# Attribute rows of two chunks side by side in a ring of 50 units: a graph network on one core

## The reference, cut to what matters

```python
for i in range(L):                       # L = 3
    q, k, v = x @ Wq[i] + bq[i], x @ Wk[i] + bk[i], x @ Wv[i] + bv[i]
    e = edge_attr_64 @ We[i]
    alpha = sum(q[dst] * (k[src] + e), -1) / sqrt(64)
    w = segment_softmax(alpha, dst)
    x = segment_sum((v[src] + e) * w[:, None], dst) + x @ Ws[i] + bs[i]
    x = relu(x)                          # and layer_norm for i < 2
...
msg = norm[:, None] * (concat([x[row], edge_attr_32], 1) @ weight)   # third layer
```

## Time and profile before

| | |
|---|---|
| median of three runs | 4897.83 us |
| the profiled execution's own time | 4912.25 us |
| its span, first to last instruction | 4910.5 us |
| mean granted TensorE clock | 0.794 |
| first gather of convolutions 0, 1, 2 | 97.8, 1285.8, 2478.2 us |
| last product of convolution 2 | 3592.6 us |

### The profile page before, as it was taken

The page is one execution under the profiler, slowest core; times in us unless marked ns, Lnnn a source line. Parts: engine busy times, 40 slices in busy tenths (PEclk is TensorE's granted clock), DMA queues, the critical chain, the costliest instruction groups (busy, mean ns, idle before and its releaser), DMA issues. The chain is left out here.

```text
span 4910.5 us, 91838 instructions
## 1 busy us (share of the span) xinstructions
PE 3513.1 (72%) x24220; PEld 3047.3 (62%) x24220; DVE 3256.5 (66%) x10240; ACT 2423.5 (49%) x8504; POOL 2498.9 (51%) x2591
## 2 busy tenths in 40 slices
PE   3677766666667666666657778777846999964887
PEld 2555555555555555555546667777746999962787
DVE  7677776777567776777737777777763333324996
ACT  0766666665376666666456666665421000000554
POOL 5777777674477777777267777777511000000000
PEclk9777888998578888988757888888757999975555
DMA  3444444442334444444144444444222000000001
GB/s 78 101 102 105 101 119 117 118 123 72 84 92 101 103 112 116 119 118 121 35 105 98 101 98 104 105 106 101 65 81 104 2 2 2 1 21 7 2 3 23
DMA packets 596225, 389.26 MB, mean 79 GB/s; under 512 B 441290, under 2 KB 518210, under 8 KB 595720
## 3 DMA queue, kind: packets, MB, share of 16 engines
q1 hardware_dynamic: 392839, 156.12, 12.5%
q0 software_dynamic: 81344, 84.68, 9.9%
q10 hardware_dynamic: 121536, 142.57, 9.8%
HBM read 315.36 MB, written 67.70 MB: 78 GB/s over the span
## 5 line engine op out<-in xcount | busy, mean ns | idle before, releaser
L615 POOL DMA_INDIRECT arena<-node_table,arena x1660 | 1603.2, 966 | 612.6 <-issue 467.8
L770 PE MATMUL ps<-arena 128*128 128x129 f32 x4980 | 948.3, 321 | 184.6 <-DVE arena L920 102.0
L679 ACT ACTIVATE arena<-arena 128x129 f32<-128x129 f32 x2490 | 742.8, 301 | 456.9 <-DVE arena L888 452.1
L770 PEld LDWEIGHTS ps<-arena 128*128 128x128 f32 x4980 | 791.0, 226 | 270.9 <-DVE arena L920 137.0
L917 DVE TENSOR_SCALAR arena<-arena 128x128 f32<-128x128 uint16 x2490 | 883.2, 360 | 94.7 <-PE ps L770 41.8
L615 POOL DMA_INDIRECT arena<-last_node_table,arena x830 | 794.1, 957 | 290.0 <-issue 233.5
L888 DVE TENSOR_TENSOR arena<-ps,arena 128x258 f32<-128x258 f32 x1245 | 524.3, 421 | 590.0 <-PE ps L759 247.9
L1165 PE MATMUL ps<-arena 128*128 128x192 bf16 x6875 | 589.6, 247 | 56.0 <-PEq L86 40.3
L1165 PEld LDWEIGHTS ps<-arena 128*128 128x128 bf16 x6875 | 587.4, 98 | 58.1 <-issue 52.3
L759 PE MATMUL ps<-arena,e 128*128 x2484 | 498.4, 332 | 113.4 <-DVE arena L888 56.5
L759 PE MATMUL ps<-arena 128*128 x2496 | 499.4, 333 | 103.6 <-ACT e L669 33.0
(11 more groups left out here) (324 smaller groups left out, 4705.8 us busy)
## 6 DMA issues: line engine op xcount, KB each, us to landing
arena<-in_attr SPq DMA_DIRECT2D x1245, 96.0 KB, 2.3
arena<-slot_rows ACTq DMA_DIRECT2D x249, 320.0 KB
edge_counts<-al ACTq DMA_DIRECT2D x397, 100.0 KB
arena<-node_table,arena POOLq DMA_INDIRECT x1660
edge_counts<-stage ACTq DMA_DIRECT2D x198, 100.0 KB
arena<-last_node_table,arena POOLq DMA_INDIRECT x830
arena<-edge_counts SPq DMA_DIRECT2D x24, 500.0 KB
stage<-edge_counts SPq DMA_DIRECT2D x16, 500.0 KB, 5.4
```

The lines of the kernel that those rows point to most:

```text
L615: pool.indirect_dma_start(out=RING[:, t % R_SLOTS, XO:XO + XG], out_offset=None, in_=table[:, :], in_offset=bass.IndirectOffsetOnAxis(ap=I ...
L679: ins = act.activation(PR[j % 3][:, q], PR[j % 3][:, q], ACT.Copy, accum_out=AL[w % 2][:, c:c + 1])
L770: ins = pe.matmul(BPS[j % 2][:, 0:AB], WOH[j % 2][:, q], RING[:, r + q, D32:D32 + AB], start=q == 0, stop=q == BT - 1)
```

## The change

The host now lays the attributes of a batch's two chunks side by side, so a partition's row is 192 words or 768 bytes and one DMA for a batch moves 128 rows of it. The ring is made of 50 units of 354 words: first the attributes of both chunks (32 + 64, 32 + 64), then the node row of the first chunk at word 192, and that of the second at word 288. `RBAT`, and with it `LEAD`, goes from 55 to 50 batches. The edge row is no longer one run of 129 columns but two runs of 65 with one distance for both chunks: the last of the 32 attributes and the 64 attributes, then the node row and its one. The first of these 130 columns meets a column of zeros in the weights and is left out when the sums are used. All tiles of `AB` columns grow from 129 to 130. Node rows are gathered as before, 256 or 264 bytes each.

```diff
-R_SLOTS = 110
-RBAT = R_SLOTS // BT
-RW = 162
-XO = D32 + D
-AB = 2 * D + 1
+RBAT = 50
+AW = D32 + D
+XO = BT * AW
+XW = D + 2
+UNIT = XO + (BT - 1) * AW + XW
+SEG = D + 1
+AB = 2 * SEG
...
-    at_v = at_d.rearrange("(g q p) f -> g p q f", q=BT, p=P)
+    at_v = at_d.rearrange("(g p) f -> g p f", p=P)
...
-            RING = V(m.take(R_SLOTS * RW), R_SLOTS, RW)
+            ring = m.take(RBAT * UNIT)
...
+                def attributes(j):
+                    return V(ring + UNIT * (j % RBAT), XO)
+
+                def nodes(j, q, n=XW):
+
+                    return V(ring + UNIT * (j % RBAT) + XO + AW * q, n)
+
+                def values(j, q0, nq):
+
+                    at = V(ring + UNIT * (j % RBAT) + AW * q0 + D32 - 1, 1)
+                    return bass.AP(tensor=at.tensor, offset=at.offset, ap=[at.ap[0]] + [[AW, nq]] * (nq > 1) + [[XO - D32 + 1, 2], [1, SEG]])
...
-                                out=RING[:, t % R_SLOTS, XO:XO + XG], out_offset=None, in_=table[:, :],
+                                out=nodes(j, q, XG), out_offset=None, in_=table[:, :],
...
-                        sp.dma_start(RING[:, r:r + BT, 0:XO], at_v[bass.ds(gs[j % REGS], 1), :, :, :].rearrange("o p q f -> (o p) q f"))\
+                        sp.dma_start(attributes(j), at_v[bass.ds(gs[j % REGS], 1), :, :].rearrange("o p f -> (o p) f"))\
...
-                            ins = pe.matmul(BPS[j % 2][:, 0:AB], WOH[j % 2][:, q], RING[:, r + q, D32:D32 + AB],
+                            ins = pe.matmul(BPS[j % 2][:, 0:AB], WOH[j % 2][:, q], values(j, q, 1),
...
-                        dve.tensor_tensor(PR[j % 3], UPS[j % 2].rearrange("p (a b) -> p a b", b=AB),
-                                          RING[:, r:r + BT, D32:D32 + AB], ALU.mult).then_inc(s["pr"], 1)
+                        dve.tensor_tensor(PR[j % 3].rearrange("p q (a b) -> p q a b", b=SEG),
+                                          UPS[j % 2].rearrange("p (q a b) -> p q a b", a=2, b=SEG), values(j, 0, BT), ALU.mult).then_inc(s["pr"], 1)
...
+    lay["attr"] = at.reshape(NG, BT, P, AW).transpose(0, 2, 1, 3).reshape(NG * P, BT * AW)
```

More of the change, by code:

```diff
@@ L613, in _ @@
                         slot_free(pool, j)
-                        for t in range(BT * j, BT * j + BT):
+                        for q in range(BT):
+                            t = BT * j + q
                             pool.indirect_dma_start(
-                                out=RING[:, t % R_SLOTS, XO:XO + XG], out_offset=None, in_=table[:, :],
+                                out=nodes(j, q, XG), out_offset=None, in_=table[:, :],
                                 in_offset=bass.IndirectOffsetOnAxis(ap=IDX[:, t:t + 1], axis=0)).then_inc(got[j % LEAD], 16)
@@ L631, in _ @@
                         slot_free(sp, j)
-                        r = (BT * j) % R_SLOTS
-                        sp.dma_start(RING[:, r:r + BT, 0:XO], at_v[bass.ds(gs[j % REGS], 1), :, :, :].rearrange("o p q f -> (o p) q f"))\
+                        sp.dma_start(attributes(j), at_v[bass.ds(gs[j % REGS], 1), :, :].rearrange("o p f -> (o p) f"))\
                             .then_inc(eld[j % LEAD], 16)
@@ L773, in aggregate @@
                             for q in range(BT):
-                                ins = pe.matmul(BPS[j % 2][:, AB:CW], WOD[j % 2][:, q], RING[:, r + q, 0:D32],
+                                ins = pe.matmul(BPS[j % 2][:, AB:CW], WOD[j % 2][:, q], attributes(j)[:, AW * q:AW * q + D32],
                                                 start=q == 0, stop=q == BT - 1)
@@ L844, in turn @@
                             o = 1024 * (i % 2) + c * P
-                            ins = pe.transpose(ps[:, o:o + P], AGG[:, 5 * i + c, 0:P], identf[:, :])
+                            ins = pe.transpose(ps[:, o:o + P], AGG[:, 5 * i + c, 1:1 + P], identf[:, :])
                         ins.then_inc(s["at"], 1)
@@ L866, in _ @@
                     if l == 0:
-                        dve.memset(RING[:, :, XO + D:XO + D + 1], 1.0)
+                        for q in range(BT):
+                            ones = V(ring, RBAT * UNIT).rearrange("p (j u) -> p j u", u=UNIT)[:, :, XO + AW * q + D:XO + AW * q + D + 1]
+                            dve.memset(ones, 1.0)
                     dve.memset(CFX[0], -BIG)
@@ L920, in weighted @@
                             ins = dve.tensor_scalar(WOD[j % 2][:, q], iota1[:, 0:P], DZT[:, t:t + 1],
-                                                    RING[:, t % R_SLOTS, RW - 1:RW], ALU.is_equal, ALU.mult)
+                                                    nodes(j, q)[:, XW - 1:XW], ALU.is_equal, ALU.mult)
                         if q == BT - 1:
@@ L997, in _ @@
                     dve.wait_ge(s["add"], T + NWIN - 1)
-                    st.link(dve.tensor_scalar(RD, AGG[:, :, 2 * D], 0.5, None, ALU.max))
-                    dve.tensor_scalar(IND, AGG[:, :, 2 * D], 0.5, None, ALU.is_gt).then_inc(s["nd"], 1)
+                    st.link(dve.tensor_scalar(RD, AGG[:, :, AB - 1], 0.5, None, ALU.max))
+                    dve.tensor_scalar(IND, AGG[:, :, AB - 1], 0.5, None, ALU.is_gt).then_inc(s["nd"], 1)
                     st.link(dve.reciprocal(RD, RD))
@@ L1623 @@
     w = {n: host["L0_gnn_" + n] for n in ("Wq", "bq", "Wk", "bk", "Wv", "We", "Ws", "bs")}
-    lay["attr"] = np.concatenate([host["edge_attr_32"], host["edge_attr_64"]], 1)
+    at = np.concatenate([host["edge_attr_32"], host["edge_attr_64"]], 1)
+    lay["attr"] = at.reshape(NG, BT, P, AW).transpose(0, 2, 1, 3).reshape(NG * P, BT * AW)
     lay["first_dst"] = host["dst"][:NG * BT * P:BT * P]
@@ L1627 @@
     lay["src_t"] = host["src"].reshape(NC, P).T
-    lay["w_edge_key"] = np.concatenate([w["We"].transpose(0, 2, 1), w["Wk"].transpose(0, 2, 1), w["bk"][:, :, None]], 2).transpose(1, 0, 2)
+    lay["w_edge_key"] = np.concatenate([np.zeros((L, D, 1), w["We"].dtype), w["We"].transpose(0, 2, 1), w["Wk"].transpose(0, 2, 1), w["bk"][:, :, None]], 2).transpose(1, 0, 2)
     lay["w_query_t"] = np.concatenate([w["Wq"], w["bq"][:, None]], 1).transpose(2, 0, 1)
```

## The result

The changed kernel takes 4927.87 us, the median of five runs (4924.98 to 4934.25), against 4903.46 us for the kernel before (4896.31 to 4906.9, five runs): a ratio of 1.0055, 95% interval 1.004 to 1.007, so 24 us or half a percent slower. Its profiled execution took 4934.25 us with a span of 4932.5 us, 22 us more than that of before. The experiments were measured in three sets. The ratios and their intervals are those of the sets of times, and can differ by a few us from the quotient of two medians.

The account below looks back on a forecast made before the run. GpSimd's unbroken gathers were taken to pace windows 0 to 4 of convolutions 0 and 1 and 0 to 7 of convolution 2, batch processing the rest. Ring 36, columns 5, semaphores -1: 40 us more, 4938 us; range 4904 to 4970.

Parts of the forecast that it names:

- The mechanism: At window ends GpSimd rests after ten gathers ahead until the first aggregation; where gathers set the pace, products wait: 25.7 us.
- ring 36: Ring of 50 batches: GpSimd's rests at window ends, passed on to the kernel's end, cost 36 us (bounds 26 and 51).
- columns 5: Wider edge row in product, aggregation and sums: 12 ns a batch over 435 processing-paced batches, 5 us (2 to 17).
- semaphores -1: End of each convolution: five semaphore clears less, 15 in all, 1 us less.
- The covers: Late windows: after windows 5 to 7 GpSimd still gathers 40 batches in time, some 2 us to spare; cost nothing.
- the rests behind them: After windows 5 to 7 of convolutions 0 and 1: GpSimd rests 15 us or more, costed at nothing.
- B: Product or TensorE's reading: breaks between the two runs cost 100 ns or more, 4980 us; chance 0.07.
- W: Experiments' rival on the edge row: the wider row in two runs costs on VectorE and TensorE; no chance given.
- C: Window ends: the rests are swallowed because late windows make them up, 4902 us; chance 0.11.
- D: Gathers: lighter descriptor traffic shortens them, at 50 ns each 41 us faster, 4857 us; chance 0.07.
- E: After windows 5 to 7: the cover is gone, 30 us more, 4968 us; chance 0.09.
- F: Attribute DMA: still cut into rows of 384 bytes, time as in the main forecast, 4938 us; chance 0.66 shared with it.

Follow-up runs that it names:

- e1: The kernel before with its own layout and a ring of 50 batches instead of 55: 4930.43 us against 4898.55, ratio 1.0058.
- e3: The changed kernel with 55 units instead of 50, the one-hots' scratch moved to make room: 4895.26 us, ratio 0.9991 to the kernel before.
- e2: The changed kernel with 53 units instead of 50, nothing else: 4893.25 us, ratio 0.9993 to the kernel before.
- e4: The kernel before with 48 batches in the ring instead of 55: 5043.51 us, ratio 1.0298.
- e11: The kernel before with 51 batches in the ring instead of 55, in the slow third set: 5887.07 us against 5913.57, ratio 0.9959.

## Why the prediction came out as it did

Forecast was 4938 us, 40 us more; measured 4927.87 us, 24 us more, inside the range and below the stated size.

*The mechanism held.* GpSimd stops after ten gathers beyond the window, in all twelve stretches, until the first aggregation. Its rests at the twelve ends sum to 27.0 us (25.7 forecast), and products wait for gathers more than before in the windows that follow. e1 shows it as the cause, without the layout.

*The sum by its terms.* Forecast was ring 36, columns 5, semaphores -1. Measured is ring 28 (20 to 37 by e1's interval) and layout with its semaphores -4 (-8 to 0 by e3's). So some 8 us of the 16 by which the forecast is too high come from each. The ring's 36 lies inside its interval; the columns' 5 (2 to 17) does not, and is the term that was mis-sized beyond doubt.

*The ring as far as window 7.* By the table, after is 36.0 us behind before there and e1 33.6. By convolution after is 4.3, 11.6 and 20.1 us behind, where the terms of the 36 come to some 9, 9 and 18. Taken against e3, the same layout with a long ring and an execution near its median, it is 40.8 us. So the size at window 7 was right to within the few us by which one profile differs from the next.

*What came back.* I let the delay of window 7 stand to the end. From window 7's last product on, the three convolutions together take 542.4 us in after and in e1, against 556.4 in before: 14 us less. Against e3 and e2, 548.4 and 550.3, it is 6 to 8 us. Half of the 14 is window 8 of convolution 2. Windows view of before, then of after, columns PE, PEld, DVE, ACT, POOL busy (count), granted clock, DMA:

```profile
3401.70:3502.30 100.60, 81.40 (x518) 74.92 (x518) 79.80 (x297) 49.92 (x191) 76.53 (x80) 0.79 0.45 99
```

```profile
3433.50:3526.70 93.20, 72.99 (x518) 67.00 (x518) 79.15 (x298) 49.66 (x191) 69.87 (x73) 0.87 0.44 104
```

The same 518 matmul records took 81.4 us at a granted clock of 0.79 and 73.0 at 0.87, and the window went from 100.6 to 93.2 us. A short ring is not needed for it: of the two other kernels with a long ring, e3 had 91.7 us at 0.87 in this window and then 67.3 us at 0.70 in the next, where before had 64.6 at 0.76, and e2 had 100.3 at 0.79 and then 58.1 at 0.94. The three kernels with a short ring do have the three shortest tails of the table (542.4, 542.4, 541.2 against 548.4 to 556.4), but with one profile of each it stays open whether the ring has to do with the clock, and how much of a delay is really made up for.

*The columns' 5 us* (2 to 17) are not there: product 4 ns longer, matmul record 1 ns shorter, and e2 and e3 at 0.9993 and 0.9991. The row of four runs that I took as the nearest (414 ns for 256 columns) was the right one; the allowance above it was too much.

*The covers held, the rests behind them were mis-sized.* Forecast were 15 us or more of rest after windows 5 to 7 of convolutions 0 and 1. The stretches after window 5 of convolution 0 and after windows 4, 5 and 6 of convolution 1 have ten gathers each:

```profile
797.91:819.53 21.62, 9.45 (x10) 0.60 0.19 46
1870.53:1890.36 19.83, 9.61 (x10) 0.76 0.27 70
1997.62:2017.24 19.62, 9.46 (x10) 0.66 0.30 77
2119.66:2138.20 18.54, 9.63 (x10) 0.78 0.33 81
```

So the rests after windows 5 and 6 are 21.62 - 12.5 = 9.1, 7.1 and 6.0 us. The forecast took the lengths of before, 28 and 29 us in convolution 1, but there GpSimd was ten batches ahead (20 gathers in the earlier trace rows), and with five spare it can't start that early. What such rests cost is read only roughly. Between the last products of windows 4 and 7 after loses 1.7 us on before in convolution 0 (580.6 against 578.0, then 953.1 against 948.8) and 4.4 in convolution 1 (584.4 against 577.2, then 957.2 against 945.6); e1 loses nothing there in sum, and against e3 after loses 13 us in the two. The 15 clears are gone.

*The rivals.* B (dear runs) and W with it fall by e2 and e3. C (rests swallowed) is refuted by e1's interval. D (shorter gathers) falls by 963 and 955 ns. What lengthens gathers was put down to VectorE's counting, although has a mean of 955 ns (340.82 / 357) where the counting is heaviest. The trace of before bears VectorE out all the same: the 243 gathers with no VectorE instruction beside them average 945 ns, the other 2247 965, and those beside lines 896 and 897, which run only in the early windows, 988 and 996. E (no cover after windows 5 to 7) wants 30 us; by the three comparisons above it is 0 to 13, the price after window 4 included, so the cover held for the most part. In e4 23 us are lost between these windows. F falls by the packets.

## What to carry to other kernels

Where a ring is filled by one engine and emptied a window later, count not its places but those beyond the window: here 55 to 50 halved them, 10 to 5, and the filling engine needed 5 to 7 (12.7 to 16.5 us at 2.5 us a batch) to work through the softmax where it sets the pace; 53 was as good as 55, 48 cost 3%. An engine that is busy half of the span can be the pace in most stretches: look for its fixed issue time and for stretches without any rest. And a delay worked out for the windows that one engine paces should not be carried undiminished through the ones that another paces.

## What the runs showed of the hardware that was not expected

- The kernel before differed by a fifth between sets (4899 against 5914 and 5955 us). In e11, of the slow third set, gathers and products are within about 1% of before's length (976 against 966 ns, 425 against 421), line 770's matmul record is 9% longer (349 against 321 ns, with a mean granted clock of 0.73 against 0.79), and engines idled for up to 41 us, in two cases 24 and 37 us of it with their inputs there, while 1 instead of 7 packets of the instruction queues moved. The cause is open.
- There, leaving out 249 of 2490 gathers brought 285 to 295 us although GpSimd was waiting for TensorE for hundreds of us, and a ring of 51 was 0.4% faster than one of 55.
- Two runs of 65 columns in place of one of 129 cost VectorE 4 ns on a product of two chunks (421 to 425) and TensorE nothing (321 to 320 ns a record).
- An indirect gather of 128 rows of 256 or 264 bytes keeps GpSimd for 945 ns (median) and 0.30 us of issue. Its mean does not follow the DMA share around it (972, 957 and 955 ns at 0.44, 0.46 and 0.48), but is 988 and 996 ns beside VectorE's lines 896 and 897.
- Attribute rows of 768 bytes in place of 384 lower the queue's share of the 16 DMA engines from 12.5% to 11.4%. They land after 2.1 us in after, e2 and e3, and those of 384 bytes after 2.1 (e1) or 2.3 us (before, e4).
